# A two-layer attention and mixture-of-experts kernel: other PSUM banks and another order for the last group's expert units, and a fill behind each scatter

## The reference, cut to what matters

```python
xn = layernorm(x)
x = x + L0_attn(xn) + L0_ffn(xn)      # gated scan with 4 decays, norm; 8 gated experts, golden-zone weights
xn = layernorm(x)
x = x + L1_attn(xn) + L1_ffn(xn)

def L1_attn(x, Wr, Wk, Wv, Wo, decay, gn_weight, gn_bias):
    r = sigmoid(x @ Wr.T); k = x @ Wk.T; v = x @ Wv.T
    scale = sigmoid(decay) ** position
    state = cumsum(k * v / scale, axis=time) * scale
    out = r * state                        # then a norm over a batch's tokens and features
    return (normed(out) * gn_weight + gn_bias) @ Wo.T

def L1_ffn(x, gate_w, expert_w, expert_b):  # 8 experts of 256x256, the best two for a token
    top_w, top_i = top_k(x @ gate_w.T, 2); top_w = softmax(top_w)
    gates = zeros((tokens, 8)); gates[token, top_i] = top_w
    return sum_e(gates[:, e] * (x @ expert_w[e] + expert_b[e]))
```

## Time and profile before

| what | us |
|---|---|
| median of 3 runs | 427.22 (426.89 to 427.35) |
| the profiled execution | 427.0 |
| its span, first to last instruction | 425.3 |
| TensorE busy | 413.8 (97%), weight loads 360.6 |
| VectorE busy | 344.0 (81%) |
| ScalarE busy | 182.6 (43%) |
| GpSimd busy | 168.9 (40%) |
| DMA | 48.97 MB, mean 115 GB/s |

### The profile page before, as it was taken

One profiled execution on the slowest core, in us unless ns is written; L12 is line 12 of the kernel. 1 busy time (PEld: TensorE's weight loads), 2 busy tenths in 40 slices (PEclk: granted clock), 3 DMA queues, 4 the chain that ended last, 5 costly groups with the idle time before them and its releaser, 6 DMA issues.

```text
span 425.3 us, 7364 instructions
## 1 busy us (share of the span) xinstructions
PE 413.8 (97%) x2456; PEld 360.6 (85%) x2456; DVE 344.0 (81%) x1073; ACT 182.6 (43%) x358; POOL 168.9 (40%) x196
## 2 busy tenths in 40 slices
PE   8999999999999999999999999999999999999992
PEld 6688888978889988878889989788889888999872
DVE  6799998898997678989966888899779666668785
ACT  4745454443263536342536143524462253524130
POOL 1556369642136102510154716010720064455662
PEclk9999999999999999999999999999999999999998
DMA  8992699970771220000021300000202933522278
GB/s 275 414 317 97 192 277 279 280 192 0 105 132 64 83 68 0 2 0 2 12 88 42 108 2 0 2 2 0 88 13 72 262 124 117 150 74 88 76 217 289
DMA packets 32453, 48.97 MB, mean 115 GB/s; under 512 B 2728, under 2 KB 26560, under 8 KB 31904
## 3 DMA queue, kind: packets, MB, share of 16 engines
q1 hardware_dynamic: 26128, 36.27, 28.0%
q0 software_dynamic: 5296, 11.42, 10.5%
q10 hardware_dynamic: 992, 0.81, 0.6%
HBM read 24.83 MB, written 23.66 MB: 114 GB/s over the span
## 4 chain that ended last, share of the span: by engine, by line
PE 81%; DVE 9%; DMA 4%; issue 2%; POOL 1%; ACT 1%; DVEq 0%; SPq 0%; POOLq 0%
PE D L740 25%; PE G L740 21%; PE U L740 21%; PE M L740 8%; DMA fetched<-returned 3%; PE D L771 1%; DVE mid_lo L1388 1%; PE M L890 1%; DVE mid L1511 1%; DVE rows L1525 1%; DVE carry_gain L1762 1%; PE M L865 1%; DMA rows<-x 1%; DVE gamma L1764 1%; PE M L763 1%
## 5 line engine op out<-in xcount | busy, mean ns | idle before, releaser
L740 PE MATMUL D<-w_hi,mid_hi 128*128 128x256 f32 x260 | 74.2, 285 | 0.2 <-DVE rows L1525 0.2
L740 PE MATMUL D<-w_hi,mid_lo 128*128 128x256 f32 x260 | 73.5, 283 | 0.0
L740 PE MATMUL D<-w_lo,mid_hi 128*128 128x256 f32 x260 | 73.5, 283 | 0.0
L1131 ACT ACTIVATE mid<-G 128x512 f32<-128x512 f32 x64 | 38.0, 596 | 69.7 <-PE G L740 44.3
L1511 DVE TENSOR_TENSOR mid<-mid,U 128x512 f32<-128x512 f32 x64 | 43.0, 684 | 22.7 <-PE U L740 10.2
L1525 DVE SCALAR_TENSOR_TENSOR rows<-D,weight,rows 128x256 f32<-128x256 f32 x128 | 54.0, 476 | 8.8 <-remote 6.3
L566 POOL TENSOR_TENSOR w_lo<-w_raw,w_hi 128x512 fp32r<-128x512 f32 x35 | 50.3, 1469 | 23.0 <-ACT w_hi L1098 12.2
L1098 ACT ACTIVATE mid_hi<-mid 128x512 fp32r<-128x512 f32 x64 | 39.9, 631 | 38.8 <-DVE mid L1511 37.0
L1388 DVE TENSOR_TENSOR mid_lo<-mid,mid_hi 128x512 fp32r<-128x512 f32 x64 | 49.4, 793 | 4.6 <-ACT mid_hi L1098 3.3
L740 PEld LDWEIGHTS D<-w_hi,mid_hi 128*128 128x128 f32 x260 | 49.7, 191 | 2.1 <-issue 1.3
L740 PE MATMUL G<-xT_hi,w_hi 128*128 128x512 f32 x126 | 50.2, 398 | 0.3 <-POOL w_lo L566 0.3
(11 more groups left out here) (360 smaller groups left out, 939.3 us busy)
## 6 DMA issues: line engine op xcount, KB each, us to landing
sorted_rows<-weighted SPq DMA_DIRECT2D x8, 1542.0 KB, 19.3
stage<-sorted_rows SPq DMA_DIRECT2D x31, 128.5 KB, 2.5
w_raw<-weights SPq DMA_DIRECT2D x2, 1280.0 KB, 14.9
w_raw<-weights SPq DMA_DIRECT2D x2, 1024.0 KB, 23.8
w_raw<-opposite POOLq DMA_DIRECT2D x2, 1024.0 KB
fetched<-returned SPq DMA_DIRECT2D x4, 512.0 KB, 7.2
rows<-x SPq DMA_DIRECT2D x7, 256.0 KB, 3.3
w_raw<-weights SPq DMA_DIRECT2D x2, 768.0 KB, 8.7
```

Of the source, the lines that this page charges most:

```text
L740: ins = nc.tensor.matmul(out_ap, a, b, start=(first and n == 0), stop=(last and n == 3 * len(pairs) - 1))
L1131: nc.scalar.activation(mid[:, c, :], GU[2 * c][:, :], ACT.Silu).then_inc(silu_ready, 1)
```

## The change

Five things change, all in the last group from its unit 4 on.

1. `WIDE_UNITS` reaches to the last unit: all units from 4 on transpose into G1 or U1 and multiply into D0 or D1. So r, k and v of the last group leave these banks: r goes to G0 and k to U0 for both halves, v to M1 and then M0. Expert pairs still use G0, U0, G1, U1 in turn.
2. The order on TensorE, ScalarE and VectorE is rewritten: r, k, v of half 0 stand between units 10 and 11, those of half 1 behind unit 12. The first four expert pairs, which stood between units 12 to 15, now follow unit 15's transposes and product. The router's last step stands behind r. P4 waits for the first half of the last adds of layer 0 only.
3. Half 1 waits until half 0's banks have been read; the waits of v, P9 and P10 for each other's banks go.
4. `return_rows` loses the extra waits of units 4 to 8.
5. Behind each scatter GpSimd writes a fill of 128x192 zeros to a spare place in SBUF (`pause`), and the next scatter waits for the fill's semaphore `paused`. (`Chain` counts a semaphore up with each instruction and makes the engine wait for it ahead of its next one.)

```diff
-WIDE_UNITS = range(4, 9)
+WIDE_UNITS = range(4, UNITS)
+PAUSE = 192
+        idle_row = w_raw[:, WHERE["down3"], 320:320 + PAUSE]
+        def late_v(h):
+            return MT[1 - h]
...
         def unit_banks(u):
             if u < WIDE_UNITS.start:
                 return MT
-            return (GU[2 + u % 2] if u in WIDE_UNITS else MT[u % 2]), DN[(u + 1) % 2]
+            return GU[2 + u % 2], DN[u % 2]
...
+            pauses = Chain(pool, paused)
+            def pause():
+                pauses(nc.gpsimd.memset(idle_row, 0.0))
             def return_rows(u):
                 tiles = UNIT_TILES[u]
                 pool.wait_ge(to_row_made, u + 1)
                 pool.wait_ge(unit_evicted, u + 1)
-                if u in (4, 5):
-                    pool.wait_ge(unit_ps, u + 3)
-                elif u in (6, 7, 8):
-                    pool.wait_ge(rkv_ps, at(LAST, 6, 2 * (u - 6) + 1))
                 for i, n in enumerate(tiles):
                     nc.gpsimd.indirect_dma_start(returned[:, :], bass.IndirectOffsetOnAxis(to_row[:, n:n + 1], 0),
                                                  made[u][:, i, :], None).then_inc(made_stored, 16)
+                    pause()
...
             def project_rkv_half(g, h):
-                for name, bank in (("r", GU[2 * h]), ("k", GU[2 * h + 1]), ("v", DN[h])):
-                    if name == "v" and h == 0:
-                        router_end(M0, 1, g)
-                    if name == "v":
-                        pe.wait_ge(unit_evicted, WIDE_UNITS.stop - 1 + h)
+                for name, bank in (("r", GU[0]), ("k", GU[1]), ("v", late_v(h))):
+                    if h:
+                        pe.wait_ge({"r": r_ready, "k": k_used, "v": logit1_read}[name],
+                                   at(g, 1, 1) if name == "v" else at(g, KC, 1))
...
+                    if name == "r" and h == 0:
+                        router_end(M0, 1, g)
...
             def unit_product(u, owners):
-                if u in (WIDE_UNITS.stop, WIDE_UNITS.stop + 1):
-                    pe.wait_ge(v_used, at(LAST, KC, u - WIDE_UNITS.stop + 1))
...
             def expert_pair(g, job):
-                if job < 4:
-                    pe.wait_ge(k_used if job % 2 else r_ready, at(g, KC, c + 1))
+                if job < 2:
+                    pe.wait_ge(k_used if job else r_ready, at(g, KC, KC))
+                elif job < 4:
+                    pe.wait_ge(unit_lo_ready, UNITS - 3 + job)
...
                     unit_transpose(5)
+                    pe.wait_ge(down_added, at(g, 2 * E, 2 * E - 1))
+                    unit_product(4, owners)
+                    unit_transpose(6)
                     pe.wait_ge(down_added, at(g, 2 * E, 2 * E))
-                    unit_product(4, owners)
-                    unit(6, owners)
+                    unit_product(5, owners)
                     unit(7, owners)
                     unit_transpose(8)
                     transpose_y(g)
                     unit_product(7, owners)
-                    unit_product(8, owners)
+                    unit(9, owners)
                     pe.wait_ge(yT_lo_ready, at(g, KC, KC))
                     logits(g)
+                    unit(10, owners)
                     project_rkv_half(g, 0)
-                    unit_transpose(9)
+                    unit(11, owners)
+                    unit(12, owners)
                     project_rkv_half(g, 1)
-                    pe.wait_ge(logit1_read, at(g, 1, 1))
-                    unit_transpose(10)
-                    unit_product(9, owners)
-                    unit(11, owners)
-                    for u in range(12, UNITS):
-                        expert_pair(g, u - 12)
+                    for u in range(13, UNITS):
                         unit(u, owners)
-                    expert_pair(g, 4)
+                    expert_pair(g, 0)
                     unit_product(UNITS - 1, owners)
-                    for job in range(5, JOBS):
+                    for job in range(1, JOBS):
                         expert_pair(g, job)
```

More of the change, by code:

```diff
@@ L359, in build @@
         made_stored = sem("made_stored")
+        paused = sem("paused")
         joined = [sem(f"joined{g}") for g in range(JOINS)]
@@ L928, in expert_pair @@
                 pair, t = job // TILES, job % TILES
-                c = (job % 4) // 2
                 if t == 0:
@@ L1208, in tanh_r_half @@
                 act.wait_ge(att_out, at(g, KC, h))
-                nc.scalar.activation(r_half[:, :], GU[2 * h][:, :], ACT.Tanh, scale=0.5).then_inc(r_ready, 1)
+                nc.scalar.activation(r_half[:, :], (GU[0] if g == LAST else GU[2 * h])[:, :], ACT.Tanh, scale=0.5).then_inc(r_ready, 1)
             def tanh_gap(g):
@@ L1318, in group @@
                     unit_out(7)
-                    unit_out(8)
+                    unit(9)
                     logits_out(g, 1)
+                    unit(10)
                     tanh_r_half(g, 0)
+                    unit(11)
                     tanh_gap(g)
-                    unit_high(9)
-                    unit_high(10)
-                    unit_out(9)
-                    unit(11)
+                    unit(12)
                     tanh_r_half(g, 1)
-                    for u in range(12, UNITS):
+                    for u in range(13, UNITS):
                         unit(u)
@@ L1533, in attention_half_start @@
                 dve.wait_ge(rkv_ps, at(g, 6, 3 * h + 2))
-                v.tensor_tensor(att_late[:, :, h, :], GU[2 * h + 1][:, :].rearrange("p (c t) -> p c t", c=KC),
+                v.tensor_tensor(att_late[:, :, h, :], GU[1][:, :].rearrange("p (c t) -> p c t", c=KC),
                                 carry_gain[:, :, :], ALU.mult).then_inc(k_used, 1)
@@ L1538, in attention_half_start @@
                 v.tensor_tensor(att_late[:, :, h, :], att_late[:, :, h, :],
-                                DN[h][:, :].rearrange("p (c t) -> p c t", c=KC), ALU.mult).then_inc(v_used, 1)
+                                late_v(h)[:, :].rearrange("p (c t) -> p c t", c=KC), ALU.mult).then_inc(v_used, 1)
             def attention_half_scan(g, h):
@@ L1899, in group @@
                     y_add(g, 0)
+                    unit_low(4)
                     stats = y_add(g, 1)
-                    unit_low(4)
                     unit_low(5)
@@ L1908, in group @@
                     y_low(g)
+                    unit_low(9)
+                    unit_low(10)
                     gates_start(g)
-                    unit_low(9)
                     attention_half_start(g, 0)
-                    gates_end(g)
-                    attention_half_start(g, 1)
-                    unit_low(10)
-                    place_one()
                     attention_half_scan(g, 0)
@@ L1918, in group @@
                     attention_half_end(g, 0)
+                    gates_end(g)
                     unit_low(12)
+                    attention_half_start(g, 1)
+                    place_one()
+                    unit_low(13)
                     attention_half_scan(g, 1)
-                    pair_add(g, 0)
-                    unit_low(13)
+                    unit_low(14)
                     attention_half_end(g, 1)
-                    pair_add(g, 1)
-                    unit_low(14)
+                    unit_low(15)
                     moments_start(g)
-                    pair_add(g, 2)
-                    unit_low(15)
-                    for job in range(3, JOBS):
+                    for job in range(JOBS):
                         pair_add(g, job)
+                        if job == 2:
+                            moments_middle(g)
                         if job == 5:
-                            moments_middle(g)
-                        if job == 8:
                             moments_end(g)
```

4 lines of the change are left out of this document (2 added, 2 removed).

## The result

The changed kernel took 431.21 us (427.89 to 432.32, 14 executions), the kernel before on the same chip 427.19 (426.57 to 430.19): a ratio of 1.008, interval 1.006 to 1.010. It is slower by 4.0 us, and the forecast was 433.4. The number lies in the range, but not for the reason that I gave, as the trace shows at once, and as the same program measured again shows still better (experiments 1 and 5: 0.9973 and 1.0009).

A forecast was written before the change was run, and what follows sets the result against it. GpSimd's scatter queue was to become the bound: 28 steps of 2.00 us land the last scatter 6.2 us later, so 427.0 + 6.2 = 433.2, as a median 433.4 us; range 426.9 to 435.6.

The forecast's parts named there:

- The period: GpSimd, start to start of successive scatters with a fill between: 2.00 us forecast, against 1.27 back to back before.
- the fourth term of the sum: GpSimd, from the fill's semaphore to the next scatter's start: 0.75 us, taken from scatters that waited on ScalarE's copy.
- the break-even point of 1.78: Spacing of scatters on GpSimd, in us, below which GpSimd keeps up and above which its queue decides the end.
- my lower bound of 1.62: Least spacing of scatters on GpSimd in us, with 0.37 from the fill's semaphore to the next scatter: 0.30 plus 0.07.
- The landing and the tail behind it: Last scatter lands at 411.87 instead of 405.66; joins, fetches, `att_low`, `project_o` and stores all move 6.2 us later.
- the fallen clock: TensorE idle 4.6 us ahead of `project_o`, its clock falling to 1.2 GHz: +8.6 us, 435.6, a rival at 8%.
- The odd wait ahead of unit 14's scatter: GpSimd waited 2.29 us where 0.75 was due; no second one in the sum, its 1.5 us kept for the upper end.
- Rival B: Fill is cheap, scatters 1.62 us apart, landing 3.3 us earlier, TensorE the later leg: 426.8 us (median 427.0), chance 25%.
- TensorE's row: TensorE's wait at P4 goes, waits at P6, P11, P13, P14 come; it ends at 419.1 instead of 417.76.
- The removed holds: Scatters of units 4 to 8 on GpSimd freed from waiting for later products: no gain, at most idle time moved.
- The Trainium skill's rule on ports: VectorE's four tensor_scalars may block scatters on GpSimd: landing up to 1.38 us later, +7.6 instead of +6.2.
- sign: Whole kernel's median: slower 0.66, within 0.85 us of no change 0.23, faster 0.11.

The follow-up runs named there:

- experiment 1: The changed kernel measured again, no edit: 425.95 us, ratio 0.9973 to the kernel before.
- experiment 5: The changed kernel measured a third time, no edit, on another chip: 425.85 us, ratio 1.0009 to the kernel before.
- experiment 6: The changed kernel with two fills behind each scatter instead of one: 433.78 us, ratio 1.0199 to the kernel before.
- experiment 9: The changed kernel with low(11) moved ahead of the scan of half 0 on VectorE: 425.15 us, ratio 0.9942 to the kernel before.
- experiment 4: The kernel before without the extra waits of units 4 to 8 in return_rows, no fills: 432.50 us, ratio 1.0141 to the kernel before.
- experiment 2: The changed kernel without the 31 fills: 430.86 us, ratio 1.0095 to the kernel before.
- 10: The changed kernel without fills, with holds on units 4, 5 and 6, and low(11) ahead of the scan: 432.60 us, ratio 1.0115 to the kernel before.
- experiment 11: The changed kernel without fills and holds, loads of units 13 to 15 held back until unit 10 is transposed: 431.63 us, ratio 1.0092 to the kernel before.
- 12: The changed kernel with fills of 128x16 instead of 128x192: 432.97 us, ratio 1.0123 to the kernel before.
- 3: The kernel before with the 31 fills alone added: 428.14 us, ratio 1.0021 to the kernel before.
- experiments 5 to 8: One chip: changed kernel unedited 425.85 us, with two fills 433.78, with holds on units 4 to 6 replacing fills 425.94; kernel before with fills, without holds 427.80.

## Why the prediction was right in the number and wrong in the reason

- **The period.** The failed step is the fourth term of the sum, "I take 0.75". It measured 0.28 in every trace with one fill, whatever its length. The sum is then 0.98 + 0.01 + 0.27 + 0.28 = 1.54 against the forecast 2.00, below the break-even point of 1.78, and even below my lower bound of 1.62, since the 0.30 of a scatter in a pair and the 0.07 behind an own semaphore don't add up. The reason that I gave ("only the signal's source differs") was the error: with the same instruction behind a wait, GpSimd's own semaphore left 0.28, and ScalarE's 0.78 in the same trace. Why the source matters so much stays open.
- **The forecast 433.4 was luck.** The late landing that its +6.2 us stand for didn't come. The first measurement reached +4.0 by another way, and in two further ones the kernel was 0.9 us faster and 0.4 slower than the one before.
- **The landing and the tail behind it.** Forecast +6.2, measured +1.0 in the first trace and -1.8 in experiment 5, where GpSimd waited for evictions again (as the text said it would if the period read 1.6). The working behind the period held: experiment 6 has a period near the one that I had assumed (1.94), and with it the last scatter (410.19, forecast 409.44), the 11.3 us to `project_o` and the fallen clock. The odd wait ahead of unit 14's scatter, which I kept out of the sum, is in every trace.
- **Rival B** described the undisturbed kernel: fill cheap, TensorE the later leg, forecast within 0.2 us of the kernel before. Measured: -0.9 and +0.4 us. It had 25%.
- **TensorE's row.** Forecast waits at P6, P11, P13, P14 of about 1.0, 0.9, 0.3, 0.2; experiment 5 has 0.70, 0.70, 0.17 and none. The wait at P4 went, as said, and P6 starts at 364.62 as forecast. The places were right, and they led to experiment 9. TensorE's end was forecast at 419.1 and came at 419.2, which is partly luck: P11 to P14 waited 0.5 less than forecast, and TensorE lost about as much in time that the sum doesn't have (it asks for low(11) at 380.5 and not 380.1).
- **The removed holds** were costed at nothing. On the chip of experiment 4, without fills, their removal cost 5.7 us. In the first measurement, with the fills at 1.53, late signals cost 2.8 us in the trace; that holds would have prevented these is likely and not shown, since no kernel of the new order with fills and holds was run. The old trace held a warning that I had not used: high(13) started at 390.75, 1.6 us after its transposes, with "remote" as the releaser. TensorE's timeline and ScalarE's, before:

```profile
388.56 0.60 PE L890 MATMUL M<-ident,stage 128*128 128x128 f32 x4
```

```profile
390.75 0.60 ACT L1098 ACTIVATE w_hi<-M 128x512 fp32r<-128x512 f32 x1 [2.30 <-remote]
```

- **The Trainium skill's rule on ports.** The prediction weighed 1.38 us by it. In the first trace a scatter started at 365.38 beside the last of the four tensor_scalars and took 1.04 instead of 0.97, and the four took 1.49 instead of 1.38. Without fills, in experiment 2, the scatter beside them took 1.07 and the four 1.37, so it wasn't the scatter that cost them 0.11. (The Trainium skill, page "SBUF — State Buffer", section "Who interferes with whom", lets one of the two block fully; these traces show 0.12 at most for a scatter (1.09, experiment 4), and don't tell whether the tensor_scalars ran in a 2-port mode.) The Trainium skill says in the same section, on SBUF's ports, that TensorE and ScalarE never wait on anyone. The late signals are no case of that: by the rows a signal was late, and no row shows an access held up.
- The **sign**, slower, came out in the first measurement through a mechanism that I had not named: late signals, and perhaps the clock behind the waits that they make. In the two others the kernel was 0.27% faster and the same.

## What to carry to other kernels

A wait that looks idle ("hold this DMA back until a later product is done") can be what keeps a burst of scatters away from something else. Where an engine that is free starts long after its input was ready, something is jammed. Compare the two times: the releaser that the profile names doesn't show it ("remote" in some of these rows, the right matmul in others). And before a spacing or a hold is credited with a cure, run the kernel without it on the same chip. And price an instruction behind a semaphore by the row with the same source of the signal, not by the one that looks most alike.

## What the runs showed of the hardware that I had not expected

- **Scatters issued too close hold up TensorE's signals, on some chips.** GpSimd's indirect scatters of 128 rows of 1 KB: at 1.27 and 1.38 us from start to start, signals of TensorE came late in experiments 2, 4, 10, 11 and 12 (out(5) 1.6 us in 2 and 2.8 in 4, high(7) 4.1 in 2), often several at once, and in 10 TensorE stopped too. At 1.53 they were late by up to 2.1 us in the first measurement, 1.27 in experiment 1 and 0.53 in 9, and on time in 3. That a wider spacing helps is shown twice on one chip: experiment 1 against 2 (4.9 us) and 9 against 10 and 12 (7.5 and 7.8 us, 12 with low(11) in another place). On the chip of experiments 5 to 8 nothing was late at 1.27, 1.53 or 1.94, so these four say nothing on the spacing, and 1.94 was not tried elsewhere. VectorE's copies start late too (0.76 in experiment 1). Where TensorE is seen to wait for VectorE's low, it starts 0.13 to 0.15 behind it in every trace, so those signals were on time. What the scatters and the signals share stays open; the loads don't matter (experiment 11), and a program that has only scatters and signals was not run.
- **The same program differs from measurement to measurement** by more than the change: the kernel before had medians of 425.45 to 427.23, the changed one of 425.85 to 431.21. A comparison on one chip gives either sign.
- **The first scatter of unit 14, the 29th here and the 53rd of the kernel,** starts 3.26 to 3.28 us behind the one before it in all 14 traces, with one fill, two or none between them. Its idle time of 2.3 us before (2.0 with a fill, 1.7 with two) is what is left of that. Nothing that it needs is outstanding. My prediction took it for an odd event; it is a fixed cost, and its cause stays open.
- **TensorE's clock** fell to 0.50 behind waits of 0.75 and 1.81 us (experiment 2), and behind one of 5.03 (experiment 6).
